# Batch norm's moments of z by ScalarE's accumulator outputs instead of VectorE's statistics, in a GNN and LSTM kernel

## What is computed

```
h = relu(adj @ (x @ Wg0 + bg0));  h = relu(adj @ (h @ Wg1 + bg1))
for p in 1..4:                       # windows of p nodes
    last hidden state of an LSTM over each window replaces the window's last node
x1 = layernorm(x + h)
agg = A_hat @ x1                     # A_hat: normalised adjacency
z   = agg @ W1.T + b1                # 256 features
h   = relu(batchnorm(z, g1, be1))    # moments over all 16384 rows
out = batchnorm(h @ W2.T + b2, g2, be2)
y   = layernorm(x1 + out)
```

## Time and profile before

| | us |
|---|---|
| median of 3 runs | 808.98 (808.69 to 810.32) |
| the profiled execution | 809.28 |
| its span, first to last instruction | 807.5 |
| PE busy | 777.1 (96%) |
| DVE busy | 720.0 (89%) |
| ACT busy | 592.3 (73%) |
| POOL busy | 114.9 (14%) |

### The profile page before, as it was taken

The page is one execution under the profiler, slowest core; times in us unless marked ns, Lnnn a source line. Parts: engine busy times, 40 slices in busy tenths (PEclk is TensorE's granted clock), DMA queues, the critical chain, the costliest instruction groups (busy, mean ns, idle before and its releaser), DMA issues.

```text
span 807.5 us, 15612 instructions
## 1 busy us (share of the span) xinstructions
PE 777.1 (96%) x4976; PEld 532.0 (66%) x4976; DVE 720.0 (89%) x1834; ACT 592.3 (73%) x1178; POOL 114.9 (14%) x125
## 2 busy tenths in 40 slices
PE   8999999999999999999999999999999988899985
PEld 5666777677767777777777777776766655344542
DVE  4787989999999999999999999999999989688996
ACT  4667777777777777777777777777867754895398
POOL 0000000000000000000000000000000001586695
PEclk9999999999999999999999999999999999999999
DMA  5010001010101010101010101010000000154245
GB/s 200 26 40 14 1 28 53 27 53 28 53 28 53 26 52 26 52 26 52 26 52 26 52 26 52 27 53 28 27 27 28 27 27 27 53 182 157 81 179 208
DMA packets 17549, 44.44 MB, mean 55 GB/s; under 512 B 2016, under 2 KB 3168, under 8 KB 17376
## 3 DMA queue, kind: packets, MB, share of 16 engines
q1 hardware_dynamic: 17504, 43.87, 15.1%
HBM read 27.09 MB, written 16.78 MB: 54 GB/s over the span
## 4 chain that ended last, share of the span: by engine, by line
PE 79%; DVE 10%; ACT 5%; issue 3%; DMA 1%; SPq 1%; POOL 1%; ACTq 0%; DVEq 0%; POOLq 0%
PE gate_bank L948 14%; PE gate_bank L949 14%; PE gate_bank L963 6%; PE gate_bank L973 6%; PE gate_bank L1020 4%; PE back_bank L902 3%; PE front_bank L858 3%; ACT z L1138 3%; PE front_bank L863 3%; PE front_bank L869 3%; PE front_bank L875 3%; PE gate_bank L932 3%; PE gate_bank L933 3%; PE gate_bank L934 3%; PE gate_bank L956 3%
## 5 line engine op out<-in xcount | busy, mean ns | idle before, releaser
L948 PE MATMUL gate_bank<-h_hi,w_hi 128*128 128x256 f16 (+2 forms) x528 | 162.7, 308 | 4.4 <-DVE h_lo L1351 2.9
L949 PE MATMUL gate_bank<-h_hi,w_lo 128*128 128x256 f16 (+2 forms) x528 | 162.5, 308 | 0.0
L1081 ACT ACTIVATE gate_i<-gate_bank,lstm_bias 128x512 f32<-128x512 f32 (+2 forms) x176 | 99.7, 567 | 62.6 <-PE gate_bank L973 32.0
L1081 ACT ACTIVATE gate_o<-gate_bank,lstm_bias 128x512 f32<-128x512 f32 (+2 forms) x176 | 100.2, 569 | 30.4 <-PE gate_bank L973 20.0
L963 PE MATMUL gate_bank<-h_lo,w_hi 128*128 128x256 f16 (+2 forms) x384 | 116.1, 302 | 0.0
L754 POOL TENSOR_TENSOR rstd<-veps,neg_half 128x8 f32<-128x8 f32 x15 | 26.3, 1753 | 630.4 <-DVE veps L1273 630.4
L948 PE MATMUL gate_bank<-s_hi,w_hi 128*128 128x256 f16 (+2 forms) x384 | 112.7, 302 | 0.6 <-DVE s_hi L1348 0.4
L949 PE MATMUL gate_bank<-s_hi,w_lo 128*128 128x256 f16 (+2 forms) x384 | 112.6, 301 | 0.0
L1334 DVE SCALAR_TENSOR_TENSOR gate_f<-gate_o,gate_f 128x512 f32<-128x512 f32 (+2 forms) x176 | 94.7, 538 | 19.2 <-ACT gate_f L1087 18.2
L1087 ACT ACTIVATE gate_f<-cell 128x512 f32<-128x512 f32 (+2 forms) x176 | 89.7, 510 | 28.5 <-DVE cell L1331 14.7
L1081 ACT ACTIVATE gate_g<-gate_bank,lstm_bias 128x512 f32<-128x512 f32 (+2 forms) x176 | 99.6, 566 | 0.7 <-PE gate_bank L956 0.2
(11 more groups left out here) (261 smaller groups left out, 1730.0 us busy)
## 6 DMA issues: line engine op xcount, KB each, us to landing
x_front<-in_x SPq DMA_DIRECT2D x16, 512.0 KB, 4.1
x_kept<-normed_sb SPq DMA_DIRECT2D x16, 512.0 KB, 2.6
z<-x_kept SPq DMA_DIRECT2D x16, 512.0 KB, 3.7
rows_sb<-in_x SPq DMA_DIRECT2D x15, 512.0 KB, 3.3
out<-z SPq DMA_DIRECT2D x15, 512.0 KB, 3.1
z<-in_wr SPq DMA_DIRECT2D x1, 1536.0 KB, 7.2
out<-z SPq DMA_DIRECT2D x2, 256.0 KB, 2.6
z<-in_wih SPq DMA_DIRECT2D x1, 192.0 KB, 2.4
```

What stands on the lines that cost most here:

```text
L948: mm(dst, w[0], v[0], start=start, stop=False)
L949: mm(dst, w[1], v[0], start=False, stop=False)
L1081: ins = activation(acts[gate][h][:, 0:n], gate_bank[h][bank_of(job, gate)][:, 0:n], ACT.Tanh if gate == "g" else ACT.Sigmoid, bias=lstm_bi ...
```

## The change

1. In the planned back stage, `z_stats` on DVE is gone. In its place stands `z_squared` on ACT, which waits for the product as the store does and follows the store in ACT's order. PE's z n + 1, the next half's tokens, and the waits behind the loop (PE's before keep_warm, DVE's before the last residual) wait for z_squared instead of z_stats.
2. The store gets an accumulator output: the sum of its row of z, into z_sum. The squaring computes (scale * bank + pivot) squared, writes it back over the bank, and its accumulator output goes into z_square. z_sum and z_square are two of the six values per chunk in z_moments.
3. The pivot is, up to sign and bias, the mean of the first chunk of each feature block: one more ACT instruction on one column behind the first two stores of half 0, with a wait of ACT for itself.
4. `early_aggregate` is now six steps (three before each of the two low parts): two reductions over 30 chunks, then the mean, its distance from the pivot, and the sum of squared differences, written as one chunk of z_moments. L1384 to L1386 are gone. The last four z keep bn_stats, and the final aggregate is the same.
5. AHEAD_OP is another table: 111 entries before, 116 after, for all streams. The other three tables and the costs stay; z_squared is planned at the store's cost and 0.05 us.

```diff
     for n in range(4):
-        after = ("back", "mixed_low", min(n, 1)) if wide else ("back", "z_stats", n - 1) if n else ("back", "mixed_low", 1)
+        after = ("back", "mixed_low", min(n, 1)) if wide else ("back", "z_squared", n - 1) if n else ("back", "mixed_low", 1)
         ops.append(("PE", ("back", "z", n), matmul_us(BANK, 3), [after]))
         ops.append(("ACT", ("back", "z_stored", n), scalar_us(BANK, 1), [("back", "z", n)]))
-        ops.append(("DVE", ("back", "z_stats", n), vector_us(BANK), [("back", "z_stored", n)]))
+        ops.append(("ACT", ("back", "z_squared", n), scalar_us(BANK, 1) + 0.05, [("back", "z", n)]))
...
 AHEAD_OP = {
...
-    ('PE', 'back', ('back', 'z', 0)): -1.25,
-    ('PE', 'back', ('back', 'z', 1)): -0.2,
-    ('ACT', 'back', ('back', 'z_stored', 1)): -0.75,
-    ('PE', 'back', ('back', 'z', 2)): -0.6,
-    ('ACT', 'back', ('back', 'z_stored', 2)): -0.7,
-    ('DVE', 'back', ('back', 'z_stats', 2)): 0.6,
+    ('PE', 'back', ('back', 'z', 0)): -1.35,
+    ('PE', 'back', ('back', 'z', 1)): -0.9,
+    ('PE', 'back', ('back', 'z', 2)): -1.25,
+    ('ACT', 'back', ('back', 'z_stored', 2)): -1.15,
     ('PE', 'back', ('back', 'z', 3)): -0.8,
-    ('ACT', 'back', ('back', 'z_stored', 3)): -0.6,
+    ('ACT', 'back', ('back', 'z_stored', 3)): -1.55,
 }
...
+                        j = n % 2
+                        first = isinstance(g, int) and (g, h) == (0, 0) and n < 2
                         wait(act, ("back", "z", n), g, h)
...
+                        if what == "z_stored":
+                            ins = activation(z[:, at, j, :].rearrange("p o n -> p (o n)"), back_to(g, h, n)[:],
+                                             ACT.Identity, bias=v1_sb[:, 0, j:j + 1], scale=1.0 / (W_SCALE * A_SCALE),
+                                             accum_out=z_sum[:, j, at])
+                            if first:
+                                ins.then_inc(first_mean, 1)
+                                act.wait_ge(first_mean, n + 1)
+                                ins = activation(pivot[:, j:j + 1], z_sum[:, j, 0:1], ACT.Identity,
+                                                 bias=v1_sb[:, 0, j:j + 1], scale=-1.0 / BANK)
+                        else:
+                            if first:
+                                wait(act, ("back", "z_stored", n), g, h)
+                            ins = activation(back_to(g, h, n)[:], back_to(g, h, n)[:], ACT.Square,
+                                             bias=pivot[:, j:j + 1], scale=1.0 / (W_SCALE * A_SCALE),
+                                             accum_out=z_square[:, j, at])
...
-                else:
-                    wait(dve, ("back", "z_stored", n), g, h)
-                    at = z_moments[:, n % 2, bass.ds(4 * g + (2 * h + n // 2), 1), :].rearrange("p o s -> p (o s)")
-                    ins = ve.bn_stats(at, back_to(g, h, n)[:])
...
+            def early_aggregate(step):
+
+                if step == 0:
+                    ve.reduce_sum(total, z_sum[:, :, 0:CHUNKS - 2], mybir.AxisListType.X)
+                    ve.reduce_sum(total_square, z_square[:, :, 0:CHUNKS - 2], mybir.AxisListType.X
+                                  ).then_inc(early_moments, 1)
+                    return
+                dve.wait_ge(early_moments, step)
+                if step == 1:
+                    ve.scalar_tensor_tensor(out=mean, in0=total, scalar=1.0 / SEEN, in1=v1_sb[:, 0, :], op0=ALU.mult,
+                                            op1=ALU.subtract).then_inc(early_moments, 1)
+                elif step == 2:
+                    ve.tensor_scalar(z_moments[:, :, CHUNKS - 3, 4], mean, 1.0 / scale, None, ALU.mult)
+                    ve.tensor_tensor(apart, mean, pivot[:], ALU.add).then_inc(early_moments, 1)
+                elif step == 3:
+                    ve.scalar_tensor_tensor(out=total, in0=apart, scalar=SEEN, in1=apart, op0=ALU.mult, op1=ALU.mult
+                                            ).then_inc(early_moments, 1)
+                elif step == 4:
+                    ve.tensor_tensor(total_square, total_square, total, ALU.subtract).then_inc(early_moments, 1)
+                else:
+                    ve.memset(z_moments[:, :, CHUNKS - 3, 3], SEEN)
+                    ve.tensor_scalar(z_moments[:, :, CHUNKS - 3, 5], total_square, 1.0 / scale ** 2, None, ALU.mult
+                                     ).then_inc(early_moments, 1)
+
-            wait(dve, ("back", "z_stats", 3), GROUPS - 1, 0)
+            wait(dve, ("back", "z_squared", 3), GROUPS - 1, 0)
...
             for n in range(2):
-                early_aggregate(n)
+                for step in range(3):
+                    early_aggregate(3 * n + step)
                 dve.wait_ge(last_mixed, n + 1)
                 high, low = agg(n)
                 ve.tensor_tensor(low, last_mix_bank[n][:], high, ALU.subtract).then_inc(last_low, 1)
-            dve.wait_ge(early_moments, 2)
-            ve.memset(z_moments[:, :, CHUNKS - 3, 3:4], BANK * (CHUNKS - 2.0))
-            ve.tensor_copy(z_moments[:, :, CHUNKS - 3, 4:5], mv[:, :, 0:1])
-            ve.tensor_scalar(z_moments[:, :, CHUNKS - 3, 5:6], mv[:, :, 1:2], BANK * (CHUNKS - 2.0), None, ALU.mult
-                             ).then_inc(early_moments, 1)
```

More of the change, by code:

```diff
@@ L209 @@
     (LSTM_JOBS[0], "high"): ((2, ("back", "tokens", 1, 1)),),
[L210 removed]
+    ("back", "tokens", 0, 0): ((1, ("back", "z_squared", 3)),),
 }
@@ new lines @@
+    ('PE', 'even', (('lstm', 3, 2), 'input', 'i')): -1.4,
+    ('PE', 'even', (('lstm', 3, 2), 'input', 'g')): -1.85,
+    ('PE', 'even', (('lstm', 3, 2), 'high', 'i')): -1.1,
+    ('PE', 'even', (('lstm', 3, 2), 'gate', 'g')): -1.4,
+    ('ACT', 'even', (('lstm', 3, 2), 'tanh')): -0.6,
+    ('DVE', 'even', (('lstm', 3, 2), 'hidden')): -0.75,
+    ('DVE', 'even', (('lstm', 3, 2), 'low')): -0.85,
+    ('DVE', 'even', (('lstm', 4, 0), 'hidden')): -1.75,
+    ('PE', 'even', (('lstm', 4, 1), 'input', 'i')): -1.65,
@@ new lines @@
+    ('DVE', 'odd', (('lstm', 3, 2), 'high')): -0.1,
+    ('DVE', 'odd', (('lstm', 3, 2), 'low')): -0.55,
+    ('PE', 'odd', (('lstm', 4, 0), 'gate', 'i')): -1.4,
+    ('DVE', 'odd', (('lstm', 4, 0), 'new')): -0.55,
+    ('DVE', 'odd', (('lstm', 4, 0), 'hidden')): -1.05,
+    ('PE', 'odd', (('lstm', 4, 1), 'input', 'i')): -1.4,
+    ('ACT', 'odd', (('lstm', 4, 1), 'act', 'i')): -1.25,
+    ('ACT', 'odd', (('lstm', 4, 1), 'act', 'o')): 0.25,
+    ('PE', 'odd', (('lstm', 4, 2), 'input', 'i')): -1.4,
@@ new lines @@
+    ('PE', 'odd', (('lstm', 4, 2), 'input', 'o')): -1.25,
+    ('DVE', 'odd', (('lstm', 4, 2), 'low')): 0.35,
+    ('PE', 'odd', (('lstm', 4, 3), 'input', 'i')): -1.0,
+    ('PE', 'odd', (('lstm', 4, 3), 'high', 'g')): -1.05,
+    ('ACT', 'odd', (('lstm', 4, 3), 'act', 'i')): -1.5,
+    ('ACT', 'odd', (('lstm', 4, 3), 'act', 'o')): -0.7,
+    ('PE', 'back', ('back', 'tokens', 0, 0)): -0.8,
+    ('PE', 'back', ('back', 'tokens', 1, 0)): -1.0,
+    ('DVE', 'back', ('back', 'residual', 1)): -0.65,
```

213 lines of the change are left out of this document (98 added, 115 removed).

## The result

The changed kernel takes 820.12 us (median of 4 runs, 819.15 to 820.26), the kernel before 809.65 us (median of 4 runs, 808.69 to 810.65). The ratio is 1.0125, 95% interval 1.011 to 1.014. I had forecast 806.8 us and a range up to 812.0: the sign was wrong and the time lies outside the range.

The account below looks back on a forecast made before the run. PE, streaming matmuls almost without pause, was taken as the loop's limit. From 809.28 us, -2.2 (late starts at z), +0.3 (end of half 14), -0.3 (early sums) and -0.3 (profiled run against median) gave 806.8 us, range 803.8 to 812.0.

Parts of the forecast that it names:

- DVE's statistics: Loop: DVE loses its statistics of z, 5.55 us a period (76.4 to 70.8); worth nothing by itself there.
- The squaring at 0.60: Loop, ACT: each added squaring takes 0.60 us like the store, 4.8 us a period.
- The accumulator output at 0.15: Loop, ACT: each accumulator output of store and squaring costs 0.15 us, 2.4 us a period (0 to 4.1).
- The bank's turn and PE's margins: Loop at z: turn 1.59 us, no quicker; new order's larger margins remove PE's late starts of 0.42 us a period, -2.2 us.
- End of half 14: Drain: 0.6 us saved before h_lo, last residual 1.2 us later behind ACT's squarings; +0.3 us taken (-0.6 to +1.2).
- Early sums: Final chain: reductions and small steps replace two early aggregates and a patch; -0.3 us (0 to 0.5 saved).
- Pivot: Near 111 us: two small ACT instructions once, with ACT waiting on itself; 0 (at most 2 x 0.5 us of ACT).
- The new order elsewhere: Fill and drain: changed orders of PE, ACT and DVE taken as 0, bounded by 2 us each way.
- C: Rival: ACT becomes late, stalls at z and the LSTM's first gate double; 812.8 us, chance 0.22.
- E: Rival: Square not in the table set with Sigmoid and Tanh, so each squaring brings table loads; about 865 us, chance 0.03.
- B: Rival: the drain gives 2.3 us more, as fewer DVE statistics there give back PE's idle time; 804.5 us, chance 0.14.
- D: Rival: nothing changes, PE streams already, stalls stay and the ends cancel; 808.7 us, chance 0.18.

Follow-up runs that it names:

- e4: The kernel before, same order, with DVE's statistics of z in the loop taken over 8 of the 512 columns; 806.63 us.
- e3: The changed kernel, same order, without the accumulator outputs of planned stores and squarings, except those of the first two stores; 811.50 us.
- e10: The changed kernel, same order, without the planned accumulator outputs and with the squarings cut to one column; 809.47 us.
- e8: The changed kernel, complete, with order entries of their own for halves 13 to 15 that bring half 14's z products earlier; 815.56 us.
- e5: The changed kernel, complete, with new order tables for the loop and halves 13 to 15, chosen with each accumulator read rated at 0.10 us; 813.01 us.
- e7: The changed kernel, same order, without the squarings' accumulator outputs, those of the stores kept; 814.26 us.
- e2: The changed kernel, same order, with the squaring cut to one column into a spare tile, both accumulator outputs kept; 811.07 us.

## Why the prediction was wrong

1. *DVE's statistics* (worth 0 by themselves). DVE fell by 4.5 us a period (76.4 to 71.9), where I had 5.55: I took durations, and back to back the statistics stand 0.61 apart. That DVE isn't the loop's limit held, though e4 shows 0.33 us a period to be had from its lateness at z, the 0.42 of step 4.

2. *The squaring at 0.60.* Right: 0.57 from its start to its read. It writes over its bank in 670 ns, where the store to SBUF takes 693. The Trainium skill's page "ScalarE: Activation LUTs", *Step-by-step: what each stage is for*, calls PSUM the quicker destination for ScalarE. The trace doesn't contradict it, by 23 ns, but doesn't show it either: the two differ in function as well, and from the start to the next start both take 0.57 us in e3. Groups by line and shape (busy us, mean ns, idle before):

```profile
L1124 ACT ACTIVATE back_bank<-back_bank,pivot 128x512 f32<-128x512 f32 x57 | 38.2, 670 | 0.2
L1113 ACT ACTIVATE z<-back_bank,v_sb 128x512 f32 x32 | 22.2, 693 | 0.6
```

3. *The accumulator output at 0.15.* Too high: 0.10 in the queue. The unit cost I feared most was smaller than I took it. ACT came to 66.9 us a period, where I had 69.7.

4. *The bank's turn and PE's margins (-2.2).* **This step failed, and it is the sum's largest.** The turn itself came as worked out: store at 239.85, matmul at 241.38, 1.53 us against 1.59. What failed is the inference from it: "The two late starts follow from the small margins, and the new ones cover the 0.26 us that the upper bound adds." The load's wait at z stayed at its size (3.8 us in 12), z's late matmuls grew from 0.42 to 0.70 us, the wait at the tokens doubled and those at L961 joined them: +1.30 us a period where I had -0.42, or +6.5 in five. I had read the larger offsets of the table as slack. They are positions, and this order was drawn up with a store without a read and a squaring at the store's cost plus 0.05: 0.57 against 0.67 with its read at the store, and 0.62 against 0.66 at the squaring. The order packs ACT's gates for two LSTM streams around z with as little slack as before, so what the plan doesn't count, arrives at PE. The measure of it: 3.4 us of squaring, which it counts, cost 0.08 us a period as long as nothing else came (e3 against e10); 1.6 us of reads, of which it counts 0.4, cost 1.24. Without the reads the new margins do cover z: in e3 the late starts at z are gone but for 0.06 us. But the saving of 0.42 doesn't reach the period even there (82.44): the order gives it away at other places, which e10 shows too (82.36 with the squarings' length gone as well). I had also written of ACT "It has the room, but not always at the right moment", and then priced only the z products by it.

5. *End of half 14 (+0.3).* **This step failed too, in place and size**: the residual is at 690.38, 11.4 us behind 678.94 where I had 1.2. 4.7 of the 11.4 come with h_lo's later end (for the most part the fill's gain and the loop's loss), 6.8 from here: 7.7 us from h_lo's end to the residual, 0.9 before. I took the z products of half 14 to stay where they were, beside the last LSTM step, and bounded the step with "a new order can bring the squarings forward". It sent them back: they waited for L1339, which the order puts behind h_lo. e8 mends that for at most 5.2 us, a part of which is the clock's. The rest can be read from the two chains, of after and e3: from the first z product to the store 1.50 against 0.86 us, so 0.64 are PE's rate, and from there to the residual 5.50 against 4.75, so 0.75 are the reads. PE's timeline in after has the slow products 0.40 to 0.43 us apart and the later ones 0.22:

```profile
683.38 0.61 PE L925 MATMUL back_bank<-rows_sb,gw_hi 128*128 128x512 f16 x1 [2.22 <-DVE rows_sb L1339]
683.78 0.63 PE L926 MATMUL back_bank<-rows_sb,gw_lo 128*128 128x512 f16 x1
...
686.68 0.38 PE L927 MATMUL gate_bank<-rows_sb,gw_hi 128*128 128x512 f16 x1
686.90 0.38 PE L925 MATMUL gate_bank<-rows_sb,gw_hi 128*128 128x512 f16 x1
```

6. *Early sums (-0.3).* Right: -0.4, from 14.6 to 14.2 us between the residual and the relu.

7. *Pivot (0).* Nearly right: two instructions of 0.29 us. But the first isn't off the chain that ended last. It stands there from 109.58 us, between the first store and the first squaring, whose bank PE waits for; with the wait for itself that is 109.55 to 109.96 us, 0.4 us at most and once, inside the bound of 1 us that I gave it.

8. *The new order elsewhere (0, within 2).* The fill gained 2.6 us, just outside my bound. It was all won before the period's stretch begins and doesn't hang on the moments: e3, e10 and after have it alike, 137.2, 136.8 and 137.2. The drain's 7.5, part of step 5, is beyond it by far. Taking "less than half of the 4.9 us that PE idles" as the bound of what an order can do was wrong: idle time bounds a gain, and nothing in the profile bounds a loss.

*The rivals.* C, ACT late, was the one that happened: the waits for ACT at L925, L905 and L961 are its sign, and its period of "82.8 and more" was passed. But I let it decide from r above 0.25, because I asked whether the bank's turn outgrows the margins. It decided at r = 0.10. At 812.8 us it was also too small, since it doubled the old stalls and gave the end 1.5 us. E, table loads, is out: the trace still has two loads of 1283 ns. B is out by the drain and D by the period. e5 comes out at 813.0 by another way than C's sum, and I make nothing of that agreement.

*What stays open.* A read behind z costs 0.05 to 0.10 us and one in the front stage 0.03 or less. Whether that is the bank's turn made longer, or that ACT's queue has less room there, no run here separates. That reads and squarings together cost more than the sum of both fits "late against the plan". It is an inference from five kernels, and e5, whose tables were chosen with the reads counted and which is still 0.77 us a period above e3, says that it may not be all. What ACT lacks there, and at which gates, I have not resolved. And e5's order is one that was found; a better one for the complete change may exist. In the order that stands the ceiling is near, though: e4 gives 2.7 us for DVE's time with nothing added to ACT. And whether PE's second stretch at 1.2 GHz in after's drain belongs to its order or to chance is open too: e3 has the same order and none there, e7 has it.

## What to carry to other kernels

In a kernel whose orders are fixed in advance, an engine at 80% may have no time to spare at the places where the order is tight: 0.10 us, sixteen times a period, of which the plan knew a quarter, cost 1.24 of its 1.6 us behind the z products, while 3.4 us that it knew cost 0.08 alone, and eight reads in the front stage 0.25 or less. In the one order chosen with the reads counted, 0.77 stayed. So ask of an added instruction whether the plan counts it before asking how long it is, and count what an option such as an accumulator output adds to the instruction stream. Before moving work to relieve a wait, shorten the work in its place (here the statistics to 8 columns, 2.7 us): it gives the ceiling of the gain in the order that stands, and the offsets of an order table don't tell how much of it is slack. And where a loop ends in a lone dependent chain, look where the new order puts the last halves' work separately from the loop: here 7.5 of 14.0 us lost lay there.

## What the runs showed of the hardware

- An accumulator output of ACT isn't free: it is an ACTIVATION_READ_ACCUMULATOR behind the instruction, 0.19 to 0.24 us long and 0.10 us from its start to the next start, for stores to SBUF, for squarings in PSUM and for the front stage's copies alike.
- Square shares a table set with Sigmoid and Tanh: two loads, before and after.
- An ACT instruction of 512 columns that squares over its own PSUM bank is recorded with 670 ns, the store from the bank to SBUF with 693; from one start to the next both take 0.57 us (e3).
- An ACT instruction on one column takes 0.14 to 0.15 us of the queue (e2, e10), so the length of the squaring is 0.42 of its 0.57 us.
- The same wait of PE at the same place, 2.22 us, is followed by the lower clock in one kernel and the higher in another. After's z products of 512 columns start 0.40 to 0.43 us apart (the level of 1.2 GHz), e3's 0.22 apart (2.4 GHz). The stretches of after, then e3, show it in the mean granted clock (the third number from the end), 0.57 and 1.00. e3's low part lay earlier, at 657 to 665 us. The wait right ahead of a matmul doesn't tell its clock.

```profile
683.00:687.00 4.00, 3.62 (x10) 1.39 (x11) 0.92 (x2) 2.12 (x7) 0.00 (x0) 0.57 0.01 4
```

```profile
677.00:680.00 3.00, 3.00 (x25) 1.74 (x23) 0.20 (x1) 2.49 (x5) 0.00 (x0) 1.00 0.01 3
```
